# Text layers of an early-fusion embedding: four layers with an attention part and a feed-forward part each, rewritten as one unrolled pipeline of 64 quads

## What is computed

```python
x = emb[tokens] + positional_encoding(Sq, D)[None]
scale = 1.0 / math.sqrt(DH)
for i in range(L):                                    # L = 4, H = 8 heads, D = 64, F = 256
    q = (x @ Wq[i] + bq[i]).reshape(B, Sq, H, DH).transpose(0, 2, 1, 3)
    k = (x @ Wv[i] + bv[i]).reshape(B, Sq, H, DH).transpose(0, 2, 1, 3)
    v = (x @ Wv[i] + bv[i]).reshape(B, Sq, H, DH).transpose(0, 2, 1, 3)
    scores = jnp.einsum('bhqd,bhkd->bhqk', q, k) * scale
    attn = jax.nn.softmax(scores, axis=-1)
    o = jnp.einsum('bhqk,bhkd->bhqd', attn, v).transpose(0, 2, 1, 3).reshape(B, Sq, D)
    x = x + layer_norm(o @ Wo[i] + bo[i], ln1_g[i], ln1_b[i])
    h = jax.nn.gelu(x @ W1[i] + b1[i], approximate=False)
    x = x + layer_norm(h @ W2[i] + b2[i], ln2_g[i], ln2_b[i])
return layer_norm(x, fin_g, fin_b)
```

## Time and profile before

| | |
|---|---|
| median of 3 runs | 2695.6 us (2692.45 to 2728.44) |
| profiled execution | 2723.24 us, its span 2721.4 us |
| PE busy | 2250.7 us, 83% of the span |
| DVE busy | 1816.3 us, 67% |
| ACT busy | 1344.1 us, 49% |
| POOL busy | 1207.3 us, 44% |
| mean granted TensorE clock | 0.904 of full speed (1.0 is 2.4 GHz, 0.5 is 1.2 GHz) |

### The profile page before, as it was taken

The page is one execution under the profiler, slowest core; times in us unless marked ns, Lnnn a source line. Parts: engine busy times, 40 slices in busy tenths (PEclk is TensorE's granted clock), DMA queues, the critical chain, the costliest instruction groups (busy, mean ns, idle before and its releaser), DMA issues. The chain is left out here.

```text
span 2721.4 us, 62098 instructions
## 1 busy us (share of the span) xinstructions
PE 2250.7 (83%) x19897; PEld 1805.2 (66%) x19897; DVE 1816.3 (67%) x5614; ACT 1344.1 (49%) x3116; POOL 1207.3 (44%) x1523
## 2 busy tenths in 40 slices
PE   5699999768886888778977888448888899699998
PEld 5699999656665766666765666436666676466665
DVE  3355565367755677467755775568888865588888
ACT  2122222125544555545554554557666655566663
POOL 2233333225546555655554554654444432443442
PEclk8899999869988999889887998759999955699999
DMA  5100000000000000000000000000000000000000
GB/s 124 29 12 17 12 17 6 1 1 1 0 1 1 1 0 0 0 2 0 0 1 1 1 0 1 0 1 0 0 0 0 0 0 1 4 10 9 8 9 11
DMA packets 39551, 19.18 MB, mean 7 GB/s; under 512 B 29508, under 2 KB 38852, under 8 KB 39366
## 3 DMA queue, kind: packets, MB, share of 16 engines
q1 hardware_dynamic: 39466, 18.00, 2.7%
HBM read 14.63 MB, written 3.36 MB: 7 GB/s over the span
## 5 line engine op out<-in xcount | busy, mean ns | idle before, releaser
L456 PE MATMUL im_c<-im_a_hi,im_w 128*128 128x256 f32 (+2 forms) x1920 | 429.4, 318 | 46.8 <-POOL im_a_lo L353 46.8
L456 PEld LDWEIGHTS im_c<-im_a_hi,im_w 128*128 128x128 f32 x1920 | 321.4, 191 | 63.3 <-POOL im_a_lo L353 47.6
L1064 POOL TENSOR_TENSOR tx_KB<-tx_KF,tx_head_rows 128x1248 fp32r<-128x1248 f32 x128 | 288.0, 2270 | 48.7 <-DVE tx_KF L932 48.7
L456 PE MATMUL im_c<-im_a_lo,im_w 128*128 128x256 f32 (+2 forms) x960 | 304.1, 317 | 0.0
L874 POOL TENSOR_TENSOR tx_rstd<-tx_var_eps,tx_power 77x4 f32<-77x4 f32 x128 | 130.7, 1021 | 369.6 <-DVE tx_var_eps L870 369.0
L1135 ACT ACTIVATE tx_PT<-tx_scores_t 77x624 f32<-77x624 f32 x256 | 175.3, 685 | 163.5 <-PE tx_scores_t L1278 154.1
L1278 PE MATMUL tx_scores_t<-tx_QP,tx_KB 128*77 128x78 f32 x2048 | 201.4, 250 | 9.9 <-DVE tx_QP L952 4.2
L946 DVE TENSOR_REDUCE tx_mpad<-tx_scores 77x8 fp32r<-77x616 f32 x256 | 202.3, 790 | 6.5 <-PE tx_scores L1260 5.9
L346 POOL TENSOR_TENSOR im_rstd<-im_var_eps,im_power 128x4 f32<-128x4 f32 x64 | 68.6, 1073 | 305.0 <-DVE im_var_eps L274 305.0
L1278 PEld LDWEIGHTS tx_scores_t<-tx_QP,tx_KB 128*77 128x77 f32 x2048 | 183.1, 157 | 29.5 <-DVE tx_QP L952 29.4
L456 PEld LDWEIGHTS im_c<-im_a_lo,im_w 128*128 128x128 f32 x960 | 182.7, 190 | 8.4
(11 more groups left out here) (312 smaller groups left out, 5977.7 us busy)
## 6 DMA issues: line engine op xcount, KB each, us to landing
im_x<-x SPq DMA_DIRECT2D x16, 384.0 KB, 3.3
out<-h_img SPq DMA_DIRECT2D x32, 64.0 KB
tx_toks<-x_txt SPq DMA_DIRECT2D x1, 1925.0 KB
im_raw<-L_tok_conv_w SPq DMA_DIRECT2D x1, 1280.0 KB, 8.9
out<-h_txt SPq DMA_DIRECT2D x32, 38.5 KB
im_raw<-L_tok_conv_w SPq DMA_DIRECT2D x1, 960.0 KB, 4.7
im_raw<-L_tok_conv_w SPq DMA_DIRECT2D x1, 640.0 KB, 6.1
tx_raw_W<-L_txt_W SPq DMA_DIRECT2D x2, 256.0 KB, 5.8
```

The source lines that it names most:

```text
L456: last = pe.matmul(acc[:, :, d0:d1], w[c][:, slot, part], img[:, b0_:b1_, d0 + shift:d1 + shift, kj:kj + J], start=opens, stop=closes)
L1064: pool.tensor_tensor(KB[:, par, t], KF[:, t].bitcast(F32).unsqueeze(1).broadcast_to([P, HPT, QW]), head_rows[:].unsqueeze(2).broadcast_to( ...
```

## The change

The loops over layers and quads are gone. Each engine runs `step(n)` for n from -2 to 69, written out in full, so 64 quads (16 for each of 4 layers) go through one pipeline, and weights are read straight from `w_all` at the quad's layer. In step n the attention is that of quad n; the output projection belongs to quad n-1, the turn before the feed-forward to n-3, `down` to n-5 and the last sum of the feed-forward to n-6. `up` and gelu run in even steps alone, for quads n-5 and n-4. `up` and `down` now write the banks `work[0]` and `work[1]`, which the projections, turns and `project_o` use too; `first_on_work0` and `first_on_work1` are the waits that guard them. The two layer norms have tiles and semaphores of their own, and rows for the feed-forward are cut into a tile `xs_f` of their own. The second layer norm takes the form of the first: gain ahead of the power, and four fused multiply-adds at the end. The arithmetic is otherwise the same. Of the diff, the parts that set the new order (functions that are merely renamed are left out; indentation is cut):

```diff
-        w_all = sb("w_all", [P, LAYERS + 1, W_COLS], F32R)
+        w_all = sb("w_all", [P, LAYERS, W_COLS], F32R)
...
+        xs_f = sb("xs_f", [P, QUAD, 2 * D], F32R)
...
+        N = LAYERS * U
+        A_NORM, F_TURN, F_DOWN, F_SUM = 1, 3, 5, 6
...
+    def scale_y(q):
+        dve.wait_ge(y_squared, q + 1)
+        dve.tensor_tensor(y_yn[:, q % 2], rows_of_work1, of(q, "ln2_g"), ALU.mult).then_inc(y_scaled, 1)
...
+    def step(n):
+        now, ahead, before = live(n), live(n + 1), live(n - 1)
+        if before:
+            normalise_o(n - 1, 3)
+        if now:
+            find_max(n, 2)
+        if ahead:
+            cut_qk(n + 1, 0)
+            cut_qk(n + 1, 1)
+        if now:
+            join_max(n, 2)
+            normalise_o(n, 0)
+            find_max(n, 3)
+        if ahead:
+            cut_qk(n + 1, 2)
+            cut_qk(n + 1, 3)
+        if live(n - F_SUM):
+            sum_y(n - F_SUM)
+        if now:
+            join_max(n, 3)
+            normalise_o(n, 1)
+        if ahead:
+            set_v(n + 1)
+        if live(n - 2):
+            sum_a(n - 2)
+        if ahead:
+            find_max(n + 1, 0)
+        if now:
+            normalise_o(n, 2)
+        if ahead:
+            join_max(n + 1, 0)
+            find_max(n + 1, 1)
+        if live(n - F_DOWN):
+            scale_y(n - F_DOWN)
+        if ahead:
+            join_max(n + 1, 1)
+        if live(n - F_DOWN):
+            var_y(n - F_DOWN)
+        if before:
+            scale_a(n - A_NORM)
+            var_a(n - A_NORM)
 
     dve.memset(out_bank[:], 0.0).then_inc(outs_cleared, 1)
     dve.memset(PT[:], 0.0).then_inc(outs_cleared, 1)
-    for rows_split in (xs, os_):
+    for rows_split in (xs, xs_f, os_):
...
-    set_attention_weights(0)
-    set_cols(0)
-    set_feed_forward_weights(0)
-    set_rows(0)
...
-        def feed_forward(g, par, first, last2, last):
-            n, ln = l * U + g, norm_at(l, g, True)
-            if first:
-                mid_sum(dve, ln - 1, 1 - par, U - 1)
-                set_attention_weights(l + 1)
-            if last:
-                dve.wait_ge(y_made, ln + 1)
-                set_cols(l + 1)
-            ln_var(dve, ln, par)
-            if not first:
-                ln_apply(dve, ln - 1, 1 - par, y_ff[1 - par])
-                end_sum(dve, ln - 1, 1 - par, g - 1, n - 1)
-            if last:
-                ln_apply(dve, ln, par, y_ff[par])
-                dve.wait_ge(w_set, l * 5 + 7)
-                for i in range(2):
-                    cut_qk(l * U + U, i, 0)
-                end_sum(dve, ln, par, g, n)
-                set_feed_forward_weights(l + 1)
-                set_rows(l + 1)
...
+    def step(n):
+        if live(n - F_TURN):
+            cut(quads(n - F_TURN), xs_f, f_hi, f_cut, n - F_TURN)
+        if live(n - 1):
+            cut(o_rows[:, (n - 1) % 2], os_, o_hi, o_cut, n - 1)
+        if live(n + 1):
+            split_k(n + 1)
+        if live(n - 1):
+            shift(n - 1, a_shift, None, "ln1_b", a_shifted)
+        if live(n + 2):
+            cut(quads(n + 2), xs, x_hi, x_cut, n + 2)
+        if live(n - F_DOWN):
+            shift(n - F_DOWN, y_shift, x_mid, "ln2_b", y_shifted)
+            power_of(n - F_DOWN, y_var_eps, y_rstd, y_var, y_power)
+        if live(n - 1):
+            power_of(n - 1, a_var_eps, a_rstd, a_var, a_power)
...
+    def gelu(q):
         for half in range(2):
-            src = (scores_t if par else scores)[:, half, 0:QW]
-            last = act.activation(HT[:, par, half], src, ACT.Gelu, bias=cols[:, 8 + half:9 + half])
-        last.then_inc(f_gelu, 1)
-
...
+    def step(n):
+        if live(n):
+            exp(n, 0)
+        if live(n - 1):
+            copy_outs(n - 1, 3)
+        if n % 2 == 0 and live(n - 5):
+            gelu(n - 5)
+        if n % 2 == 0 and live(n - 4):
+            gelu(n - 4)
+        if live(n + 1):
+            set_turned(n + 1, xT, x_turned, xT_set)
+            part_lo(n + 1, 0)
+            part_lo(n + 1, 1)
+        if live(n - 1):
+            act.wait_ge(o_set, n * QUAD)
+            hi(n - 1, o_rows[:, (n - 1) % 2], os_, o_hi)
+        if live(n - F_TURN):
+            act.wait_ge(x_mid, n - F_TURN + 1)
+            hi(n - F_TURN, quads(n - F_TURN), xs_f, f_hi)
+        if live(n):
+            exp(n, 1)
+            copy_outs(n, 0)
+        if live(n + 1):
+            part_lo(n + 1, 2)
+            part_lo(n + 1, 3)
+        if live(n):
+            exp(n, 2)
+            copy_outs(n, 1)
+        if live(n + 2):
+            if n + 2 >= U:
+                act.wait_ge(x_new, n + 2 - U + 1)
+            hi(n + 2, quads(n + 2), xs, x_hi)
+        if live(n - 1):
+            set_turned(n - 1, oT, o_turned, oT_set)
+        if live(n - F_DOWN):
+            square(n - F_DOWN, y_square, y_made, y_squared)
+        if live(n):
+            exp(n, 3)
+            copy_outs(n, 2)
+        if live(n - F_TURN):
+            set_turned(n - F_TURN, xTf[:, (n - F_TURN) % 2], f_turned, fT_set)
+        if live(n - 1):
+            square(n - A_NORM, a_square, a_made, a_squared)
+
+    act.wait_ge(outs_cleared, 5)
...
+    def first_on_work0(n):
+
+        if live(n - 1):
+            pe.wait_ge(qk_cut, n * 4)
+        if live(n - 2):
+            pe.wait_ge(oT_set, n - 1)
+        if live(n - 4):
+            pe.wait_ge(fT_set, n - 3)
+            if n % 2 == 0:
+                pe.wait_ge(f_gelu, (n - 4) * 2 + 1)
+        elif live(n - 5) and n % 2 == 0:
+            pe.wait_ge(f_gelu, (n - 5) * 2 + 1)
+
+    def first_on_work1(n):
+
+        if live(n):
+            pe.wait_ge(v_set, n + 1)
+        if live(n - 2):
+            pe.wait_ge(a_scaled, n - 1)
+        if live(n - 6):
+            pe.wait_ge(y_scaled, n - 5)
+        if n % 2 == 0 and live(n - 4):
+            pe.wait_ge(f_gelu, (n - 4) * 2 + 2)
+        elif n % 2 == 0 and live(n - 5):
+            pe.wait_ge(f_gelu, (n - 5) * 2 + 2)
+
...
+    def up(q):
         for half in range(2):
             for part in range(2):
-                last = pe.matmul((scores_t if par else scores)[:, half, 0:QW],
-                                 sec("ff1", part, half * P, (half + 1) * P),
-                                 xTf[:, par].rearrange("p b s -> p (b s)"), start=part == 0, stop=part == 1)
-        last.then_inc(f_up, 1)
...
+    def down(q):
+        pe.wait_ge(f_gelu, q * 2 + 2)
         at, end = SEC["b2"]
-        pe.matmul(y_ff[par], ones[:], w[:, at:end].unsqueeze(1).broadcast_to([P, QUAD, D]),
...
-        def feed_forward(g, par, first, last2, last):
-            n = l * U + g
-            down(n, norm_at(l, g, True), par)
-            if not last:
-                up(n + 1, 1 - par)
-            if not last2:
-                turn(xs, f_cut, f_turned, n + 2)
-            elif not last:
-                turn(xs, x_cut, x_turned, n + 2)
...
+    def step(n):
+        now, ahead, before = live(n), live(n + 1), live(n - 1)
+        even = n % 2 == 0
+        if now:
+            score_t(n, 0)
+        if before:
+            weigh(n - 1, 3)
+        if now:
+            turn_max(n, 1)
+            score(n, 2)
+        if even and (live(n - 5) or live(n - 4)):
+            pe.wait_ge(fT_set, min(n - 3, N))
+            if live(n - 2):
+                pe.wait_ge(a_scaled, n - 1)
+            elif live(n - 6):
+                pe.wait_ge(y_scaled, n - 5)
+        if even and live(n - 5):
+            up(n - 5)
+        if before:
+            turn_outs(n - 1, 3)
+        if even and now:
+            score_t(n, 1)
+            weigh(n, 0)
+        if even and live(n - 4):
+            if live(n - 5):
+                pe.wait_ge(f_gelu, (n - 5) * 2 + 2)
+            up(n - 4)
+        if ahead:
+            first_on_work0(n)
+            turn(xs, n + 1, x_cut, x_turned)
+            pe.wait_ge(xT_set, n + 2)
+            project(n + 1, 0)
+            first_on_work1(n)
+            project(n + 1, 1)
+        if now:
+            if not even:
+                score_t(n, 1)
+                weigh(n, 0)
+            turn_max(n, 2)
+            score(n, 3)
+        if ahead:
+            project(n + 1, 2)
+            project(n + 1, 3)
+        if now:
+            turn_outs(n, 0)
+            score_t(n, 2)
+            weigh(n, 1)
+            turn_max(n, 3)
+        if ahead:
+            project_v(n + 1)
+        if now:
+            turn_outs(n, 1)
+        if before:
+            if ahead:
+                pe.wait_ge(qk_cut, n * 4 + 7)
             else:
-                pe.wait_ge(w_set, l * 5 + 6)
-                pe.wait_ge(xT_set, n + 2)
-                pe.wait_ge(y_scaled, norm_at(l, g, True) + 1)
-                for i in range(2):
-                    project(n + 1, i)
-
-        turns(pe, feed_forward)
-
-
-
-        def end_at(n):
-return LAYERS * 2 * U + n
+                first_on_work0(n)
+            turn(os_, n - 1, o_cut, o_turned)
+        if now:
+            score_t(n, 3)
+        if live(n - F_DOWN):
+            if ahead:
```

(24 more changed lines are left out.)

## The result

The changed kernel takes 3187.15 us, median of 4 runs (3156.48 to 3202.51), against 2712.02 us of the kernel before on the same chip: 1.177 times as long, interval 1.161 to 1.192. The profiled execution took 3202.51 us (span 3200.6); the one of before took 2723.2. Some executions are slower, at a lower granted clock; all ratios with an interval leave them out, so they aren't exactly the quotients of the medians.

The account below looks back on a forecast made before the run. It took the order in which TensorE and VectorE hand work over as the bound. The profiled 2723 us plus 63 for longer steps and 123 for clock falls gave 2909, stated as 2880 against the median; range 2655 to 3040.

Parts of the forecast that it names:

- sum_y, four multiply-adds, stands ahead of join_max(n,3): score_t(n,3) at 15.78: VectorE, even step: sum_y's four multiply-adds, 1.42 us, precede join_max(n,3), so TensorE's score_t(n,3) comes at 15.78 us.
- The walk: Following one even and one odd step through the in-order engine queues at full clock: 38.0 us a pair, 19.0 a quad.
- GpSimd sets nothing: GpSimd's split_k is ready in both steps, at 15.25 of 17.19 us in the even one, so GpSimd delays nothing.
- one fall a pair: TensorE's clock falls once in each pair of steps, 4.1 us each, 30 x 4.1 = 123 us.
- Rival 5: Clock stays low for most of the text layers, a step about 25.5 us: 3150, anything above 2960; chance 0.12.
- up for scale_a: Even step: up(n-5) waits for the attention's gain, queued on VectorE behind join_max(n,1) and norm sums; stall 1.2 us.
- f_gelu: Even step: gelu(n-4)'s first half must read work[0] before the turn of n+1 writes it; stall 0.4 us.
- xT: Even step: the projections wait for ScalarE's copy, ready at 6.99 us; stall 0.6 us.
- turn_outs(n,0): Even step: TensorE waits for ScalarE's part_lo, copies, switch back to exp, exp(n,1) and copy_outs; stall 1.9 us.
- project_o for scale_y: Both steps: project_o needs work[1] from scale_y, queued behind normalise_o(n,2), join_max and find_max(n+1,1); stall 1.5 us.
- Rival 3: Faster: stalls overlap better and steps come near the engines' work, under 17.0 us a step, 2525 us; chance 0.13.
- rival 4: Something between, step 17.0 to 17.9 us, the change won't show: 2642 to 2700 us; chance 0.10.

Follow-up runs that it names:

- waits filled: The changed kernel plus matrix multiplications that nothing reads, put on TensorE where it would stand: 3028.7 us, 1.122 of the kernel before.
- tuned and filled: The tuned kernel plus unread matrix multiplications, 10 ahead of score_t(n,2) in even steps and 4 ahead of project_v: 2685.0 us, 0.997 of the kernel before.
- tuned: Changed kernel with scale_y and scale_a earlier, sum_y and sum_a later around join_max(n+1,1), even-step copy_outs(n,0) ahead of exp(n,1): 2760.6 us, 1.018 of the kernel before.
- sum_y late: The changed kernel with sum_y behind sum_a on VectorE, no longer ahead of join_max(n,3): 3005.0 us, 1.108 of the kernel before.
- sum_y back: The tuned and filled kernel with sum_y put back ahead of join_max(n,3): 2943.6 us, 1.094 of the kernel before.
- both, filled: Changed kernel with sum_y behind sum_a, scale_y and scale_a earlier, and unread matrix multiplications in TensorE's waits: 2877.6 us, 1.061 of the kernel before.

## Why the prediction was wrong

I said 2880 (2655 to 3040); it took 3187. The sign and the shape were right, the size was not. To the last sum of the layers the text takes 1621 us where the forecast has 1222 + 123 = 1345: 276 of the 307 us by which it was wrong. A pair is 51.2 us and not 38.0 + 4.1 = 42.1, and 30 pairs of 9.1 us more make this up.

**The step that failed** is "sum_y, four multiply-adds, stands ahead of join_max(n,3): score_t(n,3) at 15.78", with 1.42 us for the four. They take 4.79 us in the odd step and 3.10 in the even one, because GpSimd's split_k and the instructions after it run beside them. The walk had split_k's time (ready at 15.25, wanted at 17.19) and checked only whether its result was in time; "GpSimd sets nothing" was wrong. By this correction, an estimate, a pair is 38.0 + (4.79 - 1.42) + (3.10 - 1.42) = 43 us at full clock; 45.7 were measured with the waits filled, at 0.93. So of the 9.1 us this step has 5.0, the clock 5.5 - 4.1 = 1.4 (below), and 2.7 stay open. That the place is the largest part is measured: sum_y two places later gives back 170 us of text in the changed kernel and 290 in the tuned and filled one. The unrolled code itself isn't what costs: the tuned and filled kernel has it too, and takes 1184.6 us of text.

The trace of before had it. It is there at full size at a layer's end, where the gain (L898) and the sum (L901) of the last quad's feed-forward norm, all in SBUF and 0.42 us by their median, run beside the next layer's split_k (timeline):

```profile
872.98 4.67 POOL L1064 TENSOR_TENSOR tx_KB<-tx_KF,tx_head_rows 128x1248 fp32r<-128x1248 f32 x2 [2.70 <-DVE tx_KF L932]
873.33 2.19 DVE L898 TENSOR_TENSOR tx_yn<-tx_yn,tx_rows 77x256 f32<-77x256 f32 x1
...
875.56 2.37 DVE L901 TENSOR_TENSOR h_txt<-tx_yn,tx_x_shift 77x256 f32<-77x256 f32 x1
```

Smaller, it is in the 256 multiply-adds (L892, durations in ns):

```profile
L892 DVE SCALAR_TENSOR_TENSOR h_txt<-tx_yn,tx_rstd,tx_x_shift x256: 268/272/859, 626.5 to 1691.8; 77x64 f32 x96, 77x64 f32<-77x64 f32 x32
```

and one group of four with GpSimd's work beside it (timeline):

```profile
1023.76 0.73 POOL L882 TENSOR_TENSOR tx_x_shift<-h_txt,tx_rows 77x256 f32<-77x256 f32 x1
...
1024.41 1.44 DVE L892 SCALAR_TENSOR_TENSOR h_txt<-tx_yn,tx_rstd,tx_x_shift 77x64 f32 x4
...
1024.45 0.73 POOL L1057 TENSOR_TENSOR tx_xs<-h_txt,tx_xs 77x256 fp32r<-77x256 f32 x1
```

The median is 272 and the longest 859; the group of four in the earlier trace rows took 1.49 us, where four at 272 that overlap by some 80 ns are 0.86. The 0.6 us between are instructions of the four held by GpSimd's of 0.73 us. I took 1.42 as the price of the operation, and moved it beside instructions of 2.27 us. The Trainium skill states it in "SBUF — State Buffer" ("SBUF: two separate sides"): VectorE and GpSimd have one pair of SBUF ports in common, "an exclusive lock, not a bandwidth split", held for the whole instruction. VectorE needs it with two SBUF inputs, then only against a GpSimd instruction that reads SBUF, or in a mode that uses both ports. The traces agree for multiply-adds and tensor_scalar beside GpSimd's splits, cuts and shifts, with ends 0.08 and 0.05 us behind GpSimd's. They differ for its power -0.5, which reads SBUF and holds nothing. The prediction drew on two pages and not on this one.

**The clock.** I took one fall a pair at 4.1 us and gave the case that it stays low 0.12. It ran 30.7 of 51.2 us at 1.2 GHz, in two falls a pair. The price was nearer than that sounds: 5.5 us a pair given back where the waits are filled, up to 2.5 in the tuned kernel (79 us in 31 pairs). At the prediction's rate, 4.1 us for 13 at half clock, 30.7 us would have cost 9.7. Rival 5 gave 3150 and a step of 25.5 us; 25.6 came, but by luck: of the 13.2 us a pair above the walk's 38.0 only 5.5 were the clock's, and 5.0 were the hold. The rule that the prediction weighs, that idle gaps between bursts bring falls (the Trainium skill, "TensorE: Matmul & The Clock Gate", "Why this matters for your kernels"), doesn't part the cases here. The granted clock was 0.74 with no wait over 1.7 us (sum_y late), 0.84 with none over 1.5 (tuned) and 0.95 with none over 0.9, but 0.86 with waits of 3.5 (sum_y back).

**The other waits of the walk** came at their places, most of them shorter, in us: up for scale_a 1.2, measured 0.83; f_gelu 0.4, 0.46; xT 0.6, 0.52; turn_outs(n,0) 1.9, 1.33; project_v 0.9, 0.54 and that in the odd step; project_o for scale_y 1.5, 1.22 and 1.38. The 0.8 for cut_qk in the even step didn't come. The table load did:

```profile
1373.16 1.28 ACT L1042 ACT_TABLE_LOAD   x1
1374.45 0.69 ACT L1042 ACTIVATE tx_PT<-tx_scores_t 77x624 f32<-77x624 f32 x1
```

No drain, 1.29 us from load to exp, and the higher figure that the prediction quotes from the Trainium skill ("ScalarE: Activation LUTs", "What ACT_TABLE_LOAD costs") isn't seen; in the changed kernel the loads cost nothing in the end. Rival 3, faster, needed steps under 17.0 us, and said that all four engines have room. They have: 17.0 is what the tuned and filled kernel reaches, with another order on VectorE, and it is level there, as rival 4 says for such a step.

## What to carry to other kernels

Before moving an instruction, look at what the other engines run at its new place. A VectorE multiply-add, tensor_scalar or tensor_tensor that has only SBUF tensors stood behind GpSimd's tensor work here, for the rest of the running instruction and at times the whole next one; so price it by the longest of these and not by its own mean. A group whose maximum is three times its median is the sign. In an in-order queue put such work where GpSimd is idle and ahead of nothing that TensorE waits for. When waits leave TensorE thin, they can be worth more than their length: here 3.4 us of waits a pair were worth 6.6, while the clock rose from 0.69 to 0.79. It is no rule, since in "both, filled" a higher clock gained nothing.

## What the hardware did that I had not expected

- VectorE's multiply-adds with all tensors in SBUF wait for whole GpSimd instructions: 0.27 us alone, 0.75 beside one of 0.72, 2.75 beside split_k's of 2.27, the end 0.08 us after GpSimd's. A tensor_scalar with one SBUF tensor input is held as long (mean 879 ns, the multiply-adds 915).
- Not held: instructions that read PSUM, and a tensor_reduce from SBUF to SBUF (at most 418 ns beside GpSimd's x_shift, 405 alone). GpSimd's power of 1.02 us holds nothing (0.42 beside it and alone).
- Four multiply-adds in a row don't get in ahead of GpSimd's queue: the first let up to two of its instructions pass (0.44 and 2.27 us), each of the others one.
- Work that nothing reads made two kernels 79 and 161 us faster in the text layers, with a higher granted clock of TensorE (0.84 to 0.95, 0.69 to 0.93). In a third kernel the same raised the clock from 0.75 to 0.89 and gained nothing, 41.0 us a pair in both; a longer hold of sum_a took back part of it, and the rest stays open.
